# Half transposes in two row tiles: the attention transposes of a fused block, with one sine product per turn and one sum of squares

## What is computed

```python
q, k, v = split((shift_token(x) @ wqkv), 3)          # 8 heads of 64
q = l2norm(q) * qs ; k = l2norm(k) * ksc             # l2norm over the 64 of a head
q = q * cos * scale + rotate_half(q) * sin * scale   # k alike, with 1/scale
sim  = where(mask, -max, q @ k.T)                    # window of 64 tokens back
attn = softmax(sim)
x = x + (attn @ v) @ wo
h = layernorm(shift_token(x)) ; a, g = split(h @ w1 + b1, 2)
x = x + (a * gelu(g)) @ w2 + b2
```

## Time and profile before

| | |
|---|---|
| three runs | 451.48, 452.82, 452.88 us; median 452.82 |
| profiled execution | span 452.5 us (its only time; 0.3 us under the median) |
| busy over the span | PE 391.6 us (87%), DVE 342.2 (76%), ACT 299.5 (66%), POOL 205.4 (45%) |
| mean granted TensorE clock | 0.944 of full speed |

### The profile page before, as it was taken

One profiled execution on the slowest core, in us unless ns is written; L12 is line 12 of the kernel. 1 busy time (PEld: TensorE's weight loads), 2 busy tenths in 40 slices (PEclk: granted clock), 3 DMA queues, 4 the chain that ended last, 5 costly groups with the idle time before them and its releaser, 6 DMA issues.

```text
span 452.5 us, 8032 instructions
## 1 busy us (share of the span) xinstructions
PE 391.6 (87%) x2504; PEld 258.5 (57%) x2504; DVE 342.2 (76%) x1308; ACT 299.5 (66%) x986; POOL 205.4 (45%) x229
## 2 busy tenths in 40 slices
PE   0678677799999999987789888999999999867995
PEld 0456552477777767765434345767767777654442
DVE  2688747899999999984135689999999999612345
ACT  2355533589899899886432338889898998653224
POOL 6261103585775766762000066767757757410000
PEclk9988985999999999999989989999999999967898
DMA  7920000000000000000000000000000000000003
GB/s 158 292 55 2 1 1 0 0 3 1 1 2 2 0 2 1 3 0 1 0 1 0 1 0 2 0 3 2 2 0 1 3 1 1 2 1 0 0 0 93
DMA packets 10263, 7.25 MB, mean 16 GB/s; under 512 B 3245, under 2 KB 9431, under 8 KB 10222
## 3 DMA queue, kind: packets, MB, share of 16 engines
q1 hardware_dynamic: 8590, 5.63, 4.6%
q0 software_dynamic: 832, 1.12, 1.3%
q10 hardware_dynamic: 800, 0.00, 0.1%
HBM read 5.70 MB, written 1.05 MB: 15 GB/s over the span
## 4 chain that ended last, share of the span: by engine, by line
DVE 56%; PE 31%; issue 6%; ACT 4%; DMA 1%; SPq 0%; DVEq 0%; ACTq 0%
DVE pp L986 11%; PE ps L511 10%; DVE shared L971 8%; DVE ss L978 8%; DVE shared L968 7%; PE ps L618 5%; DVE kT L997 4%; PE ps L386 3%; DVE vv L1001 3%; DVE xs L1008 2%; PE ps L566 2%; PE ps L535 1%; DVE pri L993 1%; DVE nm L986 1%; DVE shared L872 1%
## 5 line engine op out<-in xcount | busy, mean ns | idle before, releaser
L386 PE MATMUL ps<-wqkv_raw,xs 128*128 128x512 f32 x192 | 108.2, 652 | 11.1 <-DVE shared L971 11.1
L340 POOL TENSOR_TENSOR pp<-pp,pri 128x512 f32<-128x512 f32 x64 | 66.6, 1041 | 94.8 <-DVE pri L993 94.8
L757 ACT ACTIVATE pp<-pp,nm 128x128 f32<-128x128 f32 x256 | 99.2, 389 | 10.3 <-DVE nm L986 10.3
L347 POOL TENSOR_TENSOR shared<-shared 128x512 f32<-128x512 f32 x64 | 81.4, 1275 | 0.0
L986 DVE CUSTOM_DVE_ANT_0 pp<-ps,msk,rr 128x128 f32<-128x128 f32 x256 | 72.4, 347 | 0.0
L511 PE MATMUL ps<-hn,w1g 128*128 128x512 f32 (+1 forms) x96 | 49.4, 637 | 5.8 <-DVE uu L1063 5.8
L757 ACT ACTIVATION_READ_ACCUMULATOR pp<-pp,nm 128x1 f32 x256 | 48.1, 188 | 0.0
L971 DVE TENSOR_TENSOR shared<-ps,stab 128x256 f32<-128x256 f32 x128 | 47.6, 413 | 0.0
L386 PEld LDWEIGHTS ps<-wqkv_raw,xs 128*128 128x128 f32 x192 | 31.1, 200 | 27.0 <-DVE shared L971 17.7
L968 DVE TENSOR_TENSOR shared<-ps,ctab 128x512 f32<-128x512 f32 x64 | 42.9, 671 | 2.5 <-ACT sqr L668 2.4
L559 PEld LDWEIGHTS ps<-pT,vv 128*64 128x64 f32 x512 | 28.2, 139 | 26.9 <-issue 24.1
(11 more groups left out here) (118 smaller groups left out, 673.1 us busy)
## 6 DMA issues: line engine op xcount, KB each, us to landing
wqkv_raw<-in_L_ffn_wqkv_dram SPq DMA_DIRECT2D x1, 1536.0 KB, 16.4
out_dram<-shared SPq DMA_DIRECT2D x4, 256.0 KB, 2.5
w_raw<-in_L_ffn_w_dram SPq DMA_DIRECT2D x1, 682.0 KB
xt<-in_x_dram SPq DMA_DIRECT2D x2, 256.0 KB, 4.5
xt<-in_x_dram SPq DMA_DIRECT2D x1, 512.0 KB, 12.4
wo_raw<-in_L_ffn_wo_dram SPq DMA_DIRECT2D x1, 512.0 KB
ct<-in_ctx_dram POOLq DMA_DIRECT2D x1, 360.0 KB, 12.2
w_raw<-in_L_ffn_w_dram SPq DMA_DIRECT2D x2, 128.0 KB
```

Source lines behind the costliest of these rows:

```text
L340: T(pp[m.j][:, a, :, :], pp[m.j][:, a, :, :], pri[m.j][:, a * 4:a * 4 + 4].unsqueeze(2).to_broadcast([128, PAIRS, 128]), ALU.mult).then_in ...
L347: T(cs[m.j][:, part], cs[m.j][:, part], sn[m.j][:, part], ALU.add).then_inc((aq_done, ak_done)[s], 1)
L386: mm(ps[:, part, :], xs[:, m.b, 0:N], wqkv_raw[:, m.layer, part * INNER:(part + 1) * INNER], start=True, stop=True).then_inc((q_ps, k_ps, ...
L757: A(pp[m.j][:, a, c, :], pp[m.j][:, a, c, :], ACT.Exp, bias=nm[m.j][:, a * 4 + c:a * 4 + c + 1], scale=-1.0, accum_out=psum_[m.j][:, a * 4 ...
```

## The change

Three things are changed in the pipelines, on the same results.

1. The eight 128x128 transposes of q and k (two groups of four) become sixteen transposes of 64 tokens by 128, in one group `rows_T(2)`: for each of eight column blocks one in the upper and one in the lower row tile of the array, into banks TQ and TK. TQ then holds the first 64 tokens of q and k, TK the last 64. `q_rows` and `k_rows` copy one bank each, as before, into one tile `rT`. The eight transposes of the weights become sixteen in one group `weights_T(1)` in the same way; `weights_out(1, 0)` and `(1, 1)` copy a bank each and now both wait for the one semaphore `pt_ps`.
2. The two sine products of a turn, 256 elements each, become one of 512, whose PSUM operand reads the halves of each head in reversed order.
3. The two sums of squares become one instruction of 1024 elements in.

```diff
@@ PE
-            def rows_T(m, s):
+            def row_tiles(t, bank, done):
+
+                for c in range(2 * PAIRS):
+                    for u, r in enumerate((slice(0, 64), slice(64, 128))):
+                        last = tr(ps[:, bank + u, c * 64:c * 64 + 64], t(c)[r, :], idn[r, r])
+                last.then_inc(done, 1)
+
+            def rows_T(m):
 
                 if m.b >= 2:
-                    pe.wait_ge(pt_ready[s], m.i - 1)
-                pe.wait_ge((aq_done, mk_done)[s], m.i + 1)
-                for c in range(PAIRS):
-                    last = tr(ps[:, TQ + s, c * 128:(c + 1) * 128],
-                              cs[m.j][:, s * INNER + c * 128:s * INNER + (c + 1) * 128], idn[:])
-                last.then_inc((qT_ps, kT_ps)[s], 1)
+                    pe.wait_ge(pt_ready[0], m.i - 1)
+                    pe.wait_ge(pt_ready[1], m.i - 1)
+                pe.wait_ge(aq_done, m.i + 1)
+                pe.wait_ge(mk_done, m.i + 1)
+                row_tiles(lambda c: cs[m.j][:, c * 128:(c + 1) * 128], TQ, rT_ps)
...
-            def weights_T(m, a):
+            def weights_T(m):
...
-                pe.wait_ge(pn_ready[a], m.i + 1)
-                for c in range(PAIRS):
-                    last = tr(ps[:, TQ + a, c * 128:(c + 1) * 128], pp[m.j][:, a, c, :], idn[:])
-                last.then_inc(pt_ps[a], 1)
+                pe.wait_ge(pn_ready[0], m.i + 1)
+                pe.wait_ge(pn_ready[1], m.i + 1)
+                row_tiles(lambda c: pp[m.j][:, c // PAIRS, c % PAIRS, :], TQ, pt_ps)
...
                 if on(2):
                     project_v(at(2))
-                    rows_T(at(2), 0)
                 if on(0):
                     out_proj(at(0))
                 if on(2):
-                    rows_T(at(2), 1)
+                    rows_T(at(2))
...
-                if on(1):
-                    weights_T(at(1), 0)
...
                 if on(2):
                     scores_(at(2))
                 if on(1):
-                    weights_T(at(1), 1)
+                    weights_T(at(1))
@@ ACT
             def weights_out(m, a):
-                act.wait_ge(pt_ps[a], m.i + 1)
-                A(pT[m.j][:, a, :, :].rearrange("p c n -> p (c n)"), ps[:, TQ + a, :], ACT.Copy).then_inc(pt_ready[a], 1)
+                act.wait_ge(pt_ps, m.i + 1)
+                A(pT[m.j][:, :, a * 64:a * 64 + 64], ps[:, TQ + a, :].rearrange("p (c n) -> p c n", n=64), ACT.Copy).then_inc(pt_ready[a], 1)
@@ DVE
-                for u in range(2):
-                    o_, i_ = slice(u * 32, u * 32 + 32), slice(32 - u * 32, 64 - u * 32)
-                    last = V.tensor_tensor(heads(sn[m.j], s)[:, :, o_], x_[:, :, i_],
-                                           stab[:, m.layer, s, o_].unsqueeze(1).to_broadcast([128, HEADS, 32]), ALU.mult)
-                last.then_inc(done, 1)
+                turned = ps[:, QB + s, :].rearrange("p (h u e) -> p h u e", u=2, e=32)[:, :, ::-1, :]
+                V.tensor_tensor(sn[m.j][:, s * INNER:(s + 1) * INNER].rearrange("p (h u e) -> p h u e", u=2, e=32), turned,
+                                stab[:, m.layer, s, :].rearrange("p (u e) -> p u e", u=2).unsqueeze(1).to_broadcast([128, HEADS, 2, 32]),
+                                ALU.mult).then_inc(done, 1)
...
+            def squared(m):
+
+                dve.wait_ge(sqq_done, m.i + 1)
+                dve.wait_ge(sqk_done, m.i + 1)
+                V.tensor_reduce(ss[m.j][:], sqr[m.j][:].rearrange("p (h d) -> p h d", d=DH), AX.X, ALU.add).then_inc(sq_sum, 1)
```

More of the change, by code:

```diff
@@ L158, in build @@
         cs, sn = (cs0, cs1), (sn0, sn1)
[L159 removed]
+        rT = sb2("rT", [128, 2 * PAIRS, N])
         vv = sb2("vv", [N, INNER])
@@ L163, in build @@
         nm, psum_, pri = (sb2(n, [128, HEADS]) for n in ("nm", "psum_", "pri"))
-        pT = [sb(f"pT{k}", [128, 2, PAIRS, 128]) for k in range(2)]
+        pT = sb2("pT", [128, 2 * PAIRS, 128])
         oT = sb2("oT", [128, PAIRS, N])
@@ L204, in build @@
         tq_done, tk_done, aq_done, ak_done, mk_done = (sem(n) for n in ("tq_done", "tk_done", "aq_done", "ak_done", "mk_done"))
-        qT_ps, kT_ps, qT_ready, kT_ready, v_ready = (sem(n) for n in ("qT_ps", "kT_ps", "qT_ready", "kT_ready", "v_ready"))
+        rT_ps, lo_ready, hi_ready, v_ready = (sem(n) for n in ("rT_ps", "lo_ready", "hi_ready", "v_ready"))
         s_ps = sem("s_ps")
-        nm_done, p_done, ri_ready, pn_ready, pt_ps, pt_ready = (
-            sem2(n) for n in ("nm_done", "p_done", "ri_ready", "pn_ready", "pt_ps", "pt_ready"))
+        pt_ps = sem("pt_ps")
+        nm_done, p_done, ri_ready, pn_ready, pt_ready = (
+            sem2(n) for n in ("nm_done", "p_done", "ri_ready", "pn_ready", "pt_ready"))
         o_ps, oT_ready, y_ps, x_upd = (sem(n) for n in ("o_ps", "oT_ready", "y_ps", "x_upd"))
@@ L534, in scores_ @@
                         r = slice(a * 64, a * 64 + 64)
-                        last = mm(ps[:, SA + a, c * 128:(c + 1) * 128], qT[m.j][r, c, :], kT[m.j][r, c, :], start=True, stop=True)
+                        last = mm(ps[:, SA + a, c * 128:(c + 1) * 128], rT[m.j][r, c, :], rT[m.j][r, PAIRS + c, :], start=True, stop=True)
                 last.then_inc(s_ps, 1)
-            def weights_T(m, a):
+            def weights_T(m):
                 if m.b + 1 < B:
-                    pe.wait_ge((qT_ready, kT_ready)[a], m.i + 2)
-                else:
-                    pe.wait_ge(pt_ready[a], m.i)
-                pe.wait_ge(pn_ready[a], m.i + 1)
-                for c in range(PAIRS):
-                    last = tr(ps[:, TQ + a, c * 128:(c + 1) * 128], pp[m.j][:, a, c, :], idn[:])
-                last.then_inc(pt_ps[a], 1)
+                    pe.wait_ge(lo_ready, m.i + 2)
+                    pe.wait_ge(hi_ready, m.i + 2)
+                elif m.i > 0:
+                    pe.wait_ge(pt_ready[0], m.i)
+                    pe.wait_ge(pt_ready[1], m.i)
+                pe.wait_ge(pn_ready[0], m.i + 1)
+                pe.wait_ge(pn_ready[1], m.i + 1)
+                row_tiles(lambda c: pp[m.j][:, c // PAIRS, c % PAIRS, :], TQ, pt_ps)
             def attend(m):
@@ L559, in attend @@
                         last = mm(ps[a * 64:a * 64 + 64, OB, c * 128:(c + 1) * 128], vv[m.j][:, h * DH:(h + 1) * DH],
-                                  pT[m.j][:, a, c, :], start=True, stop=True)
+                                  pT[m.j][:, a * PAIRS + c, :], start=True, stop=True)
                 last.then_inc(o_ps, 1)
@@ L768, in q_rows @@
             def q_rows(m):
-                act.wait_ge(qT_ps, m.i + 1)
-                A(qT[m.j][:].rearrange("p c n -> p (c n)"), ps[:, TQ, :], ACT.Copy).then_inc(qT_ready, 1)
+                act.wait_ge(rT_ps, m.i + 1)
+                A(rT[m.j][:, :, 0:64], ps[:, TQ, :].rearrange("p (c n) -> p c n", n=64), ACT.Copy).then_inc(lo_ready, 1)
             def dev_square(m):
@@ L995, in k_rows @@
             def k_rows(m):
-                dve.wait_ge(kT_ps, m.i + 1)
-                V.tensor_copy(kT[m.j][:].rearrange("p c n -> p (c n)"), ps[:, TK, :]).then_inc(kT_ready, 1)
+                dve.wait_ge(rT_ps, m.i + 1)
+                V.tensor_copy(rT[m.j][:, :, 64:128], ps[:, TK, :].rearrange("p (c n) -> p c n", n=64)).then_inc(hi_ready, 1)
             def v_rows(m):
@@ L1022, in step @@
                 if on(3):
-                    squared(at(3), 0)
-                    squared(at(3), 1)
+                    squared(at(3))
                 elif on(2):
```

11 lines of the change are left out of this document (4 added, 7 removed).

## The result

The changed kernel takes 475.76 us (median of 4 runs, 475.18 to 476.65) against 452.15 us of the kernel before on the same chip: a ratio of 1.0517, 95% interval 1.049 to 1.0544. The forecast was 472.6 us, with a range of 463 to 500.

A forecast was written before the change was run, and what follows sets the result against it. VectorE and TensorE were both taken as full, ScalarE nearly. 12 full rounds x 0.81 plus 0.2 made 9.9 us a layer, 19.8 for two; 452.5 became 472.3, plus 0.3 gave 472.6 us, range 463 to 500.

The forecast's parts named there:

- The loop: A full round from `out_proj` to the next `out_proj`, through TensorE and ScalarE: 9.14 us against 8.33, +0.81.
- value A: A half transpose takes 0.03 us with two row tiles at once, by column counts; 465 to 479 us, chance 0.50.
- the forecast's own 0.17 us without a switch: On TensorE, without a tiling change, the next group starts 0.17 us before the last one's modelled end.
- The two added switches: Into and out of `rows_T` mid-round on TensorE: the next group starts only 0.07 us before the last one's end.
- ScalarE's three items at the end of a round: Copy, squares, copy: said to start before TensorE's scores end (158.90), the first copy needing only the first four weight transposes.
- VectorE's saving vanishes: The merged VectorE instructions save 0.24 us a round, lost since VectorE has 8.1 us of work in 9.1.
- VectorE stays the bound: Rival: the loop from `out_proj` to `out_proj` is under 8.09 us, 6.7 us saved, 446 us; chance of faster 0.05.
- taken together as +0.2: The last three rounds of a layer: -0.15, +0.19 (the one with `hidden`) and +0.18 us against the kernel before.
- Filling the pipeline: 0: The filling of the pipeline was to add no time: 0 us.
- the hole and the late copies: TensorE waits some 0.4 us before `variance`; ScalarE's first weight copy starts 5.36 us after `out_proj`, against 4.1.
- The rival of a fallen clock: TensorE's clock halves for a tenth of the rounds' work: some +20 us, 490; the band 479 to 499 had 0.32.

The follow-up runs named there:

- squares ahead: The changed kernel with ScalarE's squares of q moved ahead of the first copy of the transposed weights: 463.47 us, ratio 1.0237.
- `deviation` ahead: The changed kernel with `deviation` ahead of `project_q` on TensorE and `dev_square` ahead of the squares of k on ScalarE: 468.49 us, ratio 1.0342.
- the merges alone: The kernel before with only the one sine product and the one sum of squares: 448.72 us, ratio 0.9891; again 449.06 us, 0.9921.
- both moves: The changed kernel with `deviation` ahead of `project_q`, `dev_square` ahead of k's squares, and q's squares ahead of both weight copies: 454.12 us, ratio 1.0029.

## Why the prediction was right, step by step

- *The loop.* Forecast 9.14 us a round for value A, measured 9.18. From `out_proj`: `rows_T` 0.99 (1.01), `project_q` 1.64 (1.66), `deviation` 2.50 (2.62), `variance` 3.25 (3.37), scores 3.67 (3.79), the weights' transposes 4.60 (4.79), first copy 5.36 (5.48), `attend` 7.15 (7.20). Two small sizes were off: a projection behind tiles takes 0.96 and not 0.86 to the next group, as one behind `attend` did before (161.31 to 162.27 in the earlier trace rows), and the transposes behind the scores start 1.00 and not 0.93 after them; the forecast's own 0.17 us without a switch, taken from the scores' 1.16, would have given 0.99. The two added switches are as forecast, 0.07 us (158.31 against 158.38) and 0.06 (158.96 against 159.02). So the transposes came 0.19 late and `attend` only 0.05, since two errors cancelled: the sixteen are shorter than worked out (0.66 us for 0.72), and the second copy follows the squares after 0.48 us and not 0.58. The 0.04 us of the round is in this part luck. That the items are really in the loop was shown by taking two of them out (squares ahead: -0.48; `deviation` ahead: -0.50; both: -0.99). One reading of the forecast was wrong without harm: of ScalarE's three items at the end of a round only the first copy (158.47) starts before the scores are over at 158.90; the squares start at 158.94 and the second copy at 159.53.
- *A half transpose.* Value A, 0.03 us: sixteen take 0.71 and 0.66 us with a last one of 0.22, so 0.033 and 0.029 each; once the group runs, both tiles start one every 0.062 us. The weight load of a half transpose is 138 ns, about that of a whole one (141 in the earlier trace rows); the next line, from the loads by form between 111 and 190 us, shows it. The Trainium skill's rule for a weight load, columns over 1.2 ("TensorE: Matmul & The Clock Gate", section "LDWEIGHTS (loading the stationary operand)"), gave an estimate of 53 ns per instruction for two tiles at once; here the trace disagrees, at 29 to 33 ns.

```profile
L520 PEld LDWEIGHTS ps<-idn,shared 64*128 64x128 f32 x144 | 5.2, 138 | 1.1
```

- *VectorE's saving vanishes.* Right in the rounds. The reason given was too small: it vanishes in the kernel before as well, since TensorE's list was full there (the merges alone: rounds unchanged). The rival of 446 us, "VectorE stays the bound", rested on 0.24 us a round that the kernel before could not have given either.
- *The ends of the layers* were the term that failed: "taken together as +0.2" for the last three rounds. In layer one they take 25.44 us for 23.97, +1.47, and so they do in both layers of the other profiled execution of the change. Of this, 0.39 us are in the middle one at full clock, where 0.19 was forecast (the step is right and too small), and 1.08 in the last, where 0.18 was forecast and the clock is granted at 0.80 (220 to 228 us) against 1.00 before (212 to 219); how much of the 1.08 is the clock no run separates. In layer two it is 27.01 for 26.40, at clocks of 0.55 and 0.56 in the last round. The way from the last `heads_out` of layer one to the first of layer two, for which the sum has nothing, takes 62.87 us for 60.82; its part from 227.9 to 272 us, the feed-forward, ran at a clock of 0.89, where the kernel before had 0.96 from 219.17 to 262. "Filling the pipeline: 0" did not come out either, the first `heads_out` is 2.63 us earlier (92.29 for 94.92), but that is the clock of that execution and not the change: in the other one, with 0.76 of the clock from 60 to 95 us as in the kernel before, it is 95.32. The sum between the two profiled executions: 19.9 us for the 24 full rounds (19.4 forecast), 2.1 for the last rounds (0.4 forecast), 2.05 between the layers, 0.3 behind the last `heads_out`, -2.6 at the start, together 21.6 against 19.8. The rounds were forecast by their mechanism; that the rest came out within 2 us is in part luck, as terms of 2 us and more stand against each other.
- *Which part costs it.* I put it all on the hole and the late copies. The experiments give the late weights' transposes 0.96 us a round by themselves (whole ones) and the group of q and k behind `out_proj` 0.29; with whole transposes and everything together it is 1.43, and the half transposes return 0.57, which makes the 0.86. The two parts make 1.25; the 0.18 up to 1.43 no run assigns, and the common wait of both copies, which was never tried alone, is in it. That q's transposes had stood in free time ahead of `out_proj` was not in my account; in the full change that loss is not seen apart, since `attend` to `out_proj` became shorter by the same group.
- *The clock.* In the full rounds it stayed at 2.4 GHz, as taken. The rival of a fallen clock was priced for the wrong place: it falls at the ends of the layers, and without the change too. The last round of layer two was at half clock before (9.25 us for 6.82 in layer one) and after (9.48 for 7.90).

Left open: half transposes for the weights at their two old places were not tried. In the kernel each row tile writes a bank of its own, so that both groups would need TQ and TK, the second while ScalarE still copies the first; the program gives a use to all eight banks.

## What to carry to other kernels

When several engines each have a full list, a saving on one can be worth nothing in the steady rounds (here 0.24 us of VectorE's work, and the round stayed at 8.32), and the price of a reordering is read by following one loop from an instruction to itself a round later, across the engines; here that gave the round to 0.04 us and then, turned round, a kernel that is faster than before. Merging two groups of work into one makes its consumers wait for the later of the two: ask what stands behind those consumers, and move from there whatever is ready early into the new wait. Then look at the ends of a pipeline as well, where waits that cost nothing in themselves were followed by a lower clock of TensorE in the stage behind them.

## What the runs showed of the hardware that was not expected

- A transposing weight load of 128 fp32 columns is 141 ns (whole) and 138 ns (64 rows), against 187 to 191 for an fp32 matmul of the same columns; and in two row tiles at once half transposes start every 0.029 to 0.033 us on the mean, the shortest distance of any group here.
- TensorE's clock fell behind rounds in which no wait was longer than 1.3 us. With waits of 1.27, 0.82 and 0.70 us in the round, the granted clock was 0.65 in the 18 us from 208 to 226 with both moves; with 0.78, 1.12 and 0.70 it was 0.94 there with the merges alone; throw-away matmuls in the waits held it at 1.00, and were worth some 11 us (454.12 to 442.73, on two chips) in a kernel of 450.
- The same kernel can be granted different clocks in the same stage: the change had 0.89 and 0.76 from 60 to 95 us in its two profiled executions, and its first `heads_out` came at 92.29 and 95.32 us.
